# Attention values by plain fp32 products instead of split halves, and a deeper store-and-load ring for the exponentials

## What is computed

```python
xn = group_norm(x, gamma, beta)
xf = xn.reshape(B, n, C)                      # n = 1024 pixels, C = 128 channels
q = xf @ Wq + bq; k = xf @ Wk + bk; v = xf @ Wv + bv
attn = jnp.einsum('bnc,bmc->bnm', q, k) * scale
attn = jax.nn.softmax(attn, axis=-1)
out = jnp.einsum('bnm,bmc->bnc', attn, v)
out = out @ Wp + bp
return xn + out.reshape(B, H, W, C)
```

## Time and profile before

| | |
|---|---|
| median of 3 runs | 1132.37 us (1132.25 to 1133.01) |
| the profiled execution | 1129.47 us |
| its span in the trace | 1127.7 us |
| TensorE, VectorE, ScalarE, GpSimd busy | 86%, 80%, 66%, 63% of the span |
| mean granted TensorE clock | 0.964 of 2.4 GHz |

### The profile page before, as it was taken

How to read it: one execution, slowest core, us unless ns; L and a number is a source line. 1 busy time by engine, 2 the same in 40 slices (tenths; PEclk the granted TensorE clock), 3 DMA queues, 4 the chain that set the end, 5 groups by cost and what they waited for, 6 DMA issues and landing times.

```text
span 1127.7 us, 20253 instructions
## 1 busy us (share of the span) xinstructions
PE 965.2 (86%) x6068; PEld 852.9 (76%) x6068; DVE 905.2 (80%) x1628; ACT 749.6 (66%) x1402; POOL 714.5 (63%) x494
## 2 busy tenths in 40 slices
PE   5979988897979889898888989889798988999865
PEld 4867877686868778787777878778687887877754
DVE  7758977978888798787879888797988879887752
ACT  2467747767767676766767677676776767687532
POOL 5425684756848575694847659475675856665645
PEclk9999999999999999899998999999999998999987
DMA  6003637447262744637365363735636374456673
GB/s 103 3 1 94 175 86 188 122 141 181 83 184 84 201 134 117 173 87 207 85 180 152 105 158 102 204 103 158 167 91 169 96 199 124 118 159 191 192 209 94
DMA packets 177797, 152.87 MB, mean 136 GB/s; under 512 B 77792, under 2 KB 161248, under 8 KB 177760
## 3 DMA queue, kind: packets, MB, share of 16 engines
q1 hardware_dynamic: 176912, 152.03, 49.7%
q10 hardware_dynamic: 848, 0.39, 0.2%
HBM read 76.87 MB, written 75.50 MB: 135 GB/s over the span
## 4 chain that ended last, share of the span: by engine, by line
POOL 36%; issue 33%; DMA 6%; DVE 3%; PE 3%; SPq 1%; ACT 1%; POOLq 1%; DVEq 0%; ACTq 0%
POOL et_lo L1449 16%; POOL g_lo L1449 4%; POOL d L1455 4%; DMA e_by_keys<-e_blocks 3%; POOL r_tok L1508 3%; DMA e_blocks<-e 2%; POOL h_lo L1449 2%; POOL xn_lo L1449 2%; POOL t_lo L1449 2%; POOL r_tok L1511 2%; SPq L410 1%; DVE et_f L1934 1%; PE work L528 1%; PE work L530 1%; PE work L529 1%
## 5 line engine op out<-in xcount | busy, mean ns | idle before, releaser
L1449 POOL TENSOR_TENSOR et_lo<-et_f,et_hi 128x1024 fp32r<-128x1024 f32 x128 | 313.9, 2464 | 251.3 <-ACT et_hi L1073 251.3
L1934 DVE STREAM_TRANSPOSE et_f<-e_by_keys 128x1024 f32<-128x1024 f32 x128 | 157.5, 1237 | 103.6 <-DMA e_by_keys<-e_blocks 103.3
L528 PE MATMUL work<-t_lo,wc_hi 128*128 128x256 f32 x576 | 168.8, 293 | 10.3 <-DVE nm L1841 7.4
L528 PE MATMUL work<-et_lo,vv_hi 128*128 128x256 f32 x512 | 152.1, 297 | 16.5 <-POOL et_lo L1449 16.0
L530 PE MATMUL work<-t_hi,wc_hi 128*128 128x256 f32 x576 | 162.4, 282 | 0.0
L529 PE MATMUL work<-t_hi,wc_lo 128*128 128x256 f32 x576 | 162.0, 281 | 0.0
L1073 ACT ACTIVATE et_hi<-et_f 128x1024 fp32r<-128x1024 f32 x128 | 133.6, 1055 | 29.4 <-DVE et_f L1934 29.4
L529 PE MATMUL work<-et_hi,vv_lo 128*128 128x256 f32 x512 | 148.1, 289 | 0.0
L530 PE MATMUL work<-et_hi,vv_hi 128*128 128x256 f32 x512 | 148.0, 289 | 0.0
L1066 ACT ACTIVATE e<-ps_s,nm 128x1024 f32<-128x1024 f32 x64 | 71.4, 1115 | 80.2 <-DVE et_f L1934 76.7
L528 PEld LDWEIGHTS work<-t_lo,wc_hi 128*128 128x128 f32 x576 | 109.3, 190 | 17.1 <-DVE nm L1841 12.0
(11 more groups left out here) (183 smaller groups left out, 2743.3 us busy)
## 6 DMA issues: line engine op xcount, KB each, us to landing
e_blocks<-e SPq DMA_DIRECT2D x512, 128.0 KB, 2.6
e_by_keys<-e_blocks SPq DMA_DIRECT2D x128, 512.0 KB, 4.1
x_in<-in_x SPq DMA_DIRECT2D x64, 128.0 KB, 4.4
out<-r_tok SPq DMA_DIRECT2D x32, 256.0 KB, 2.4
w_up_t<-in_L_conv_w_up SPq DMA_DIRECT2D x1, 384.0 KB, 3.7
const<-in_const ACTq DMA_DIRECT2D x1, 166.0 KB, 4.5
y<-in_L_conv_w_up ACTq DMA_DIRECT2D x1, 128.0 KB, 4.5
y<-in_L_conv_w_qkv SPq DMA_DIRECT2D x1, 128.0 KB, 4.8
```

The lines of the kernel that those rows point to most:

```text
L528: te.matmul(dst, wh, xl, start=first, stop=False)
L1449: return pool.tensor_tensor(dst, full, hi, ALU.subtract)
L1934: dve.transpose(et_f[:, :, cols_].rearrange("p b (q j) -> p q b j", q=4), e_by_keys[t % 2][:, :].rearrange("p (q b j) -> p q b j", q=4, b= ...
```

## The change

`values` uses one plain fp32 product where it had three of fp32r, so the halves of the exponentials (`et_hi`, `et_lo`) and of the values (`vv_hi`, `vv_lo`) are no longer made; `vv_half` copies the values once, and `residual` needs one addition instead of two. The room of the two halves holds eight transposed tiles (`et`) instead of four, so `et_turn` of the next image waits only for the values that read the same two tiles. The blocks in memory get four places instead of two. `exp(n, t)` waits for the store of tile t - 2 and for the transpose of tile t - 3 (t - 2 for the last tile), where it waited for the transpose of t - 2. A tile is stored by one DMA of 512 KB, in another order of the queries within the tile, which `a_part` undoes with a strided write. The load of tile t follows the store of tile t + 1 on SyncE's queue. The lists of all engines and the plans of the banks are written anew. In TensorE's list for the fill, `make_weights` moves behind the first five convolutions. The diff, without the plans, the semaphores' declarations, the fill, the drain, and VectorE's and GpSimd's lists for a turn:

```diff
--- before.py
+++ after.py
@@ -203,17 +203,14 @@
         near = placed("near", [128, 2, 3, D], qq_at)
         kk_hi, kk_lo = (sb(f"kk_{p}", [128, PIX], F32R) for p in ("hi", "lo"))
         vv_at = region("vv_mem", 2 * TILES * 128)
-        vv_hi, vv_lo = (placed(f"vv_{p}", [128, TILES, 128], vv_at + 4 * TILES * 128 * k, F32R)
-                        for k, p in enumerate(("hi", "lo")))
+        vv_t = placed("vv_t", [128, TILES, 128], vv_at)
         nm1 = sb("nm1", [128, TILES])
         sum1 = sb("sum1", [128, TILES])
         rec1 = sb("rec1", [128, TILES])
         e = [sb(f"e_{k}", [128, PIX]) for k in range(2)]
         e_by_keys = [sb(f"e_by_keys_{k}", [128, PIX]) for k in range(2)]
         et_at = region("et_mem", 2 * TILES * HALF)
-        et_hi, et_lo = (placed(f"et_{p}", [128, TILES, HALF], et_at + 4 * TILES * HALF * k, F32R)
-                        for k, p in enumerate(("hi", "lo")))
-        et_f = placed("et_f", [128, TILES, HALF], et_at + 4 * TILES * HALF)
+        et = placed("et", [128, TILES, PIX], et_at)
         wc_f = placed("wc_f", [128, NT, 3, D], et_at)
         w_up1_t = placed("w_up1_t", [128, 3, D], et_at + 4 * NT * 3 * D)[:, :, :]
         diag = placed("diag", [128, 2, 3, 3, 128], et_at + 4 * (NT + 1) * 3 * D)
...
@@ -360,7 +355,7 @@
         wl1 = r_tok[:, :, :]
         wv_t = wl1[:, 2, :]
 
-        e_blocks = nc.dram_tensor("e_blocks", (2, 128 * PIX), F32, kind="Internal").ap()
+        e_blocks = nc.dram_tensor("e_blocks", (4, 128 * PIX), F32, kind="Internal").ap()
...
@@ -405,35 +400,33 @@
 
             def move_out(n, t):
                 sp.wait_ge(*e_ready.after(n, t))
-                blocks = e_blocks[t % 2].rearrange("(a j q m) -> q j a m", a=4, j=32, q=4)
-                for part in range(4):
-                    sp.dma_start(blocks[part], e[t % 2][32 * part:32 * (part + 1), :].rearrange("j (a m) -> j a m", a=4)) \
-                      .then_inc(written[t % 2].handle, 16)
+                sp.dma_start(e_blocks[t % 4].rearrange("(a q m) -> q a m", a=4, q=128),
+                             e[t % 2][:, :].rearrange("q (a m) -> q a m", a=4)).then_inc(written[t % 2].handle, 16)
 
             def move_in(n, t):
                 sp.wait_ge(*written[t % 2].after(n, t // 2))
-                sp.dma_start(e_by_keys[t % 2][:, :], e_blocks[t % 2].rearrange("(p c) -> p c", p=128)) \
+                sp.dma_start(e_by_keys[t % 2][:, :], e_blocks[t % 4].rearrange("(p c) -> p c", p=128)) \
                   .then_inc(moved[t % 2].handle, 16)
...
@@ -441,79 +434,79 @@
             def turn_program(it):
                 a, b, c, d = it, it + 1, it + 2, it + 3
                 move_out(a, 0)
+                move_out(a, 1)
                 move_in(a, 0)
-                move_out(a, 1)
+                move_out(a, 2)
                 move_in(a, 1)
-                move_out(a, 2)
                 move_out(a, 3)
                 move_in(a, 2)
+                move_out(a, 4)
                 move_in(a, 3)
-                load_x(d)
-                move_out(a, 4)
                 move_out(a, 5)
                 move_in(a, 4)
+                load_x(d)
+                move_out(a, 6)
                 move_in(a, 5)
-                move_out(a, 6)
                 move_out(a, 7)
+                store(a, 0)
                 move_in(a, 6)
                 move_in(a, 7)
-                store(a, 0)
                 store(a, 1)
...
@@ -680,13 +673,13 @@
 
             def values(n, j):
 
-                cols_ = slice((j % 2) * 256, (j % 2 + 1) * 256)
-                te.wait_ge(*et_lo_ready.after(n, 2 * j + 1))
-                te.wait_ge(*vv_lo_ready.after(n, 1))
+                pixels_ = slice(j * 256, (j + 1) * 256)
+                te.wait_ge(*et_ready.after(n, 2 * j + 1))
+                te.wait_ge(*vv_ready.after(n, 1))
                 te.wait_ge(*bank_free("pv", j, n))
                 for kt in range(TILES):
-                    mm = mm3(bank("pv", j, n)[:, 0:256], (vv_hi[:, kt, :], vv_lo[:, kt, :]),
-                             (et_hi[:, kt, cols_], et_lo[:, kt, cols_]), kt == 0, kt == TILES - 1)
+                    mm = te.matmul(bank("pv", j, n)[:, 0:256], vv_t[:, kt, :], et[:, kt, pixels_],
+                                   start=kt == 0, stop=kt == TILES - 1)
                 mm.then_inc(pe["pv"].handle, 1)
...
@@ -1051,31 +1044,28 @@
                 act.activation(kk_hi[:, k * HALF:(k + 1) * HALF], bank("kk", k, n)[:, :], ACT.Identity, bias=bk1) \
                    .then_inc(kk_hi_ready.handle, 1)
 
-            def vv_hi_half(n, k):
+            def vv_half(n, k):
                 act.wait_ge(*pe["vv"].after(n, k))
-                act.wait_ge(*v_sum_ready.after(n - 1, k))
+                act.wait_ge(*r_tok_ready.after(n - 1, k))
                 act.wait_ge(*pe["pv"].after(n - 1, 3))
-                act.activation(vv_hi[:, 4 * k:4 * k + 4, :], bank("vv", k, n)[:, :].rearrange("p (t c) -> p t c", t=4),
-                               ACT.Copy).then_inc(vv_hi_ready.handle, 1)
+                act.activation(vv_t[:, 4 * k:4 * k + 4, :], bank("vv", k, n)[:, :].rearrange("p (t c) -> p t c", t=4),
+                               ACT.Copy).then_inc(vv_ready.handle, 1)
 
             def exp(n, t):
                 act.wait_ge(*max1_ready.after(n, t))
-                act.wait_ge(*et_ready.after(n, t - 2))
+                act.wait_ge(*written[t % 2].after(n, t // 2 - 1))
+                act.wait_ge(*et_ready.after(n, t - 3 if t < TILES - 1 else t - 2))
                 if t % 4 == 0:
                     act.wait_ge(*rec1_ready.after(n - 1, t // 4))
                 act.activation(e[t % 2][:, :].rearrange("p (a b i) -> p b a i", a=4, b=TILES),
                                score_tile(n, t)[:, :].rearrange("p (b a i) -> p b a i", a=4, b=TILES), ACT.Exp,
                                bias=nm1[:, t:t + 1], accum_out=sum1[:, t:t + 1]).then_inc(e_ready.handle, 1)
 
-            def et_hi_tile(n, t):
-                cols_ = slice((t % 4) * 128, (t % 4 + 1) * 128)
-                act.wait_ge(*et_ready.after(n, t))
-                act.activation(et_hi[:, :, cols_], et_f[:, :, cols_], ACT.Copy).then_inc(et_hi_ready.handle, 1)
-
             def a_part(n, j):
                 act.wait_ge(*pe["pv"].after(n, j))
                 act.wait_ge(*pe["pj"].after(n, j // 2 - 1))
-                act.activation(a_all[:, (j % 2) * 256:(j % 2 + 1) * 256], bank("pv", j, n)[:, 0:256], ACT.Copy) \
+                pixels_ = a_all[:, (j % 2) * 256:(j % 2 + 1) * 256].rearrange("p (t i q) -> p t q i", t=2, q=4)
+                act.activation(pixels_, bank("pv", j, n)[:, 0:256].rearrange("p (t q i) -> p t q i", t=2, q=4), ACT.Copy) \
                    .then_inc(a_ready.handle, 1)
 
             def scale_biases():
...
@@ -1492,23 +1442,15 @@
                 minus(xn_lo[:, cols_], y[:, cols_], xn_hi[:, cols_].bitcast(F32)).then_inc(xn_lo_ready.handle, 1)
 
 
-            def et_lo_tile(n, t):
-                cols_ = slice((t % 4) * 128, (t % 4 + 1) * 128)
-                pool.wait_ge(*et_hi_ready.after(n, t))
-                minus(et_lo[:, :, cols_], et_f[:, :, cols_], et_hi[:, :, cols_].bitcast(F32)).then_inc(et_lo_ready.handle, 1)
-
             def residual(n, k):
                 four = slice(4 * k, 4 * k + 4)
-                pool.wait_ge(*vv_lo_ready.after(n, k))
+                pool.wait_ge(*vv_ready.after(n, k))
                 pool.wait_ge(*stored.after(n, k - 1))
                 if is_first(n) and k == 0:
                     pool.wait_ge(*w1_ready.after(0, 0))
                     pool.wait_ge(*vp_ready.after(0, 0))
                     pool.wait_ge(*biases_ready.after(0, 0))
-                pool.tensor_tensor(r_tok[:, :, :], vv_hi[:, four, :].bitcast(F32), vv_lo[:, four, :].bitcast(F32), ALU.add) \
-                    .then_inc(v_sum_ready.handle, 1)
-                pool.wait_ge(*v_sum_ready.after(n, k))
-                pool.tensor_tensor(r_tok[:, :, :], r_tok[:, :, :], bp_row[:, :].rearrange("p (a c) -> p a c", a=1)
+                pool.tensor_tensor(r_tok[:, :, :], vv_t[:, four, :], bp_row[:, :].rearrange("p (a c) -> p a c", a=1)
...
@@ -1910,12 +1812,6 @@
                 biased_lo(kk_lo[:, cols_], bank("kk", k, n)[:, :], bk1, kk_hi[:, cols_].bitcast(F32)) \
                     .then_inc(kk_lo_ready.handle, 1)
 
-            def vv_lo_half(n, k):
-                dve.wait_ge(*vv_hi_ready.after(n, k))
-                dve.tensor_tensor(vv_lo[:, 4 * k:4 * k + 4, :], bank("vv", k, n)[:, :].rearrange("p (t c) -> p t c", t=4),
-                                  vv_hi[:, 4 * k:4 * k + 4, :].bitcast(F32), ALU.subtract) \
-                   .then_inc(vv_lo_ready.handle, 1)
-
             def row_max(n, t):
                 dve.wait_ge(*pe["s"].after(n, t))
                 dve.wait_ge(*e_ready.after(n - 1, t))
@@ -1928,10 +1824,8 @@
                 if is_first(n) and t == 0:
                     dve.wait_ge(*g_lo_ready.after(1, 3))
```

(90 more changed lines are left out.)

706 lines of the change are left out of this document (311 added, 395 removed), and 58 rows, old and new, of tables (BANK_PLAN, DRAIN_PLAN, FILL_PLAN).

## The result

The change makes the kernel faster: 1008.53 us (median of 4 runs, 1007.76 to 1009.9) beside 1132.69 us for the kernel before on the same chip, a ratio of 0.8901 (95%: 0.8884 to 0.8918). I had forecast 1091 us with a range of 1060 to 1135.

The account below looks back on a forecast made before the run. No engine was full, so waits, mostly TensorE's, were taken as the bound. Twelve pipeline turns at -2.3 us (-28), the end -10 and the fill -2 took the profiled 1129.5 us to 1089; forecast 1091, range 1060 to 1135.

Parts of the forecast that it names:

- the sum of the waits: TensorE's waits for exp, `u`, `et_lo` and `vv_lo`, 5.1 us a turn: four fifths would go, -4.1 us.
- The term of -0.7 for the clock: TensorE: half of the 1.4 us a turn lost to low granted clock comes back with fewer gaps.
- The plain product: `values` on TensorE: 0.433 us a key tile instead of 0.356, adding 2.5 us a turn, up to 3.5.
- four passes: Products in `values`: by the skill's rule 0.476 us each, turn +3.8 us, 1107 us in all; chance 0.08.
- Line 1797: VectorE's update of `u`: stretched to 1919 ns by contention with GpSimd's `et_lo`; near 0.7 us without it.
- The loop of exps: ScalarE's exp, store, load, VectorE's transpose: a pair of tiles takes 7.7 us instead of 11.1.
- The end: Last image: faster exp pairs and no `et_hi` wait, less costlier values and unhidden earlier ones; together -10 us.
- The fill: Start of the kernel: five convolutions before `make_weights` gain 2 us, bounds 0 and 5.
- The single store: SP's queue: one 512 KB store issues sooner but lands later; 0.8 us less to 0.7 more, taken as zero.
- The orders: Lists of all engines and bank plans: moves not costed singly; 2 us allowed, for the fill.
- TensorE runs nearly full: Rival: all 5.1 us of waits, 1 us more and the low clock go; -5.0 a turn, 1057 us; chance 0.17.
- The waits come back elsewhere: Rival: load behind the next exp keeps VectorE waiting; about 0 a turn, some 1120 us; chance 0.19.

Follow-up runs that it names:

- a_load_next: Changed kernel, but in full turns, tiles 3 to 7, exp waits for the transpose of t-2 and each load follows its own store: 1139.85 us.
- p_halves_kept: Kernel before with one plain fp32 product of the high halves per key tile, all halves still made and waited for: 1131.76 us, ratio 1.0022.
- p_no_et_lo: p_halves_kept without GpSimd's low half of the exponentials, values waiting for ScalarE's high half instead: 1081.02 us, ratio 0.9568 to the kernel before.
- runs with six and ten tiles: Changed kernel with values summed over six key tiles, or ten (first two repeated), instead of eight: 994.81 and 1048.49 us.
- p_memset: p_halves_kept with GpSimd's low-half subtraction replaced by a constant fill of similar length that reads nothing: 1102.37 us, ratio 0.9760 to the kernel before.
- p_plain_only: Kernel before with the plain fp32 products alone, halves gone; loop, four stores and orders as before: 1077.02 us, ratio 0.9556.
- a_four_stores: Changed kernel with each tile stored by four transfers of 128 KB instead of one of 512 KB: 1054.95 us, ratio 0.9317 to the kernel before.
- r_ring_only: Kernel before with the new loop, four blocks and single store; halves and all orders but SyncE's as before: 1247.67 us, ratio 1.1054.
- pr_old_orders: Changed kernel's plain products and new loop, with the kernel before's engine orders (except SP) and bank plans: 1196.81 us, ratio 1.0607 to the kernel before.
- a_gpsimd_work: Changed kernel with eight unused GpSimd subtractions a turn put back about where the low halves stood: 1080.81 us, ratio 0.9586 to the kernel before.

## Why the prediction was wrong

**The step that failed is the sum of the waits:** "of the 5.1 us of named waits I take four fifths, -4.1, since a wait removed usually uncovers the next", and before it "The other 3.1 us of idle time a turn are waits of the local attention and of the output projection, which the change does not name". Idle time was to fall from 8.17 to 4.1 us a turn; it fell to 0.35. That is 3.7 us a turn, 41 us in eleven. The reason lies in how I had chosen the waits: by the engine that TensorE waited for last. The subtraction on GpSimd stretched VectorE's updates and delayed GpSimd's own later work, and an exp that waits holds ScalarE's list (a_load_next); both come out on TensorE as waits for `pt` or `a_all`, which I had put down as not concerned. In p_halves_kept, where the subtraction stands, and then in p_no_et_lo, where it alone is gone, these two are:
```profile
PE work L623 <- ACT pt L1032: 15.3, 11, 1.4
...
PE work L664 <- ACT a_all L1078: 5.6, 11, 0.5
```
```profile
PE work L664 <- ACT a_all L1078: 1.6, 6, 0.4
PE work L623 <- ACT pt L1032: 1.5, 3, 0.7
```
By parts: the plain products, with the halves' end, took the turn from 66.84 to 62.25 us, -4.6, where their terms made about +0.5 (+2.5, and four fifths of the 27.2 us for `u`, `et_lo` and `vv_lo`, -2.0); loop, single store and orders together took it on to 58.62, -3.6, where four fifths of the waits for exp made -2.1. The term of -0.7 for the clock belongs to both.

With the 24 us of busy time below, 12.2 of the fill and 5.8 of the end, less the 2.3 of a twelfth turn that I had counted, these 41 make 81 us; between the 1089 that I forecast for the profiled execution and its 1009.1 lie 80.

**The plain product.** Its price was right: 0.433 us a key tile predicted; the calls give 2 x 0.216 to 2 x 0.222 = 0.43 to 0.44. The Trainium skill (FP8 and Floating Point Precision, TensorE Precision Notes) says that true FP32 takes four passes; four at fp32r's 0.119 us would be 0.476 us a key tile, an estimate, and the calls show less. But I added the price to the path in full, +2.5 us a turn, and alone it costs nothing that can be told (ratio 1.0022). Of the busy time that I forecast, 58.67 + 2.5 - 0.7 = 60.5 us a turn, 58.27 was measured: 24 us in eleven turns. About 8 of the 24 are the clock, 1.00 instead of the half that I gave back. Where the other 16 went is not shown: busy time isn't the sum of the records' prices, as the runs with six and ten tiles show (3.53 us of records taken out lower it by 2.62, added they raise it by 3.15), but with the product alone it is 60.02 us, near the forecast, and it doesn't shrink where waits go with the subtraction (60.14 in p_memset, 60.07 in p_no_et_lo).

**Line 1797.** Right, in cause and size: 1919 to 715 ns, and p_memset shows that the subtraction's reading was it. What I did not see is what the time in GpSimd's queue costs, another 21 us.

**The loop of exps.** I had 7.7 us for a pair of tiles in the last image. The exps of one parity there, against the earlier trace rows:
```profile
958.66 1.11 ACT L1060 ACTIVATE e<-ps_t,nm 128x1024 f32<-128x1024 f32 x1 [1.82 <-DVE et L1828]
...
966.41 1.11 ACT L1060 ACTIVATE e<-ps_t,nm 128x1024 f32<-128x1024 f32 x1 [3.53 <-DVE et L1828]
...
974.13 1.11 ACT L1060 ACTIVATE e<-ps_t,nm 128x1024 f32<-128x1024 f32 x1
...
986.52 1.11 ACT L1060 ACTIVATE e<-ps_t,nm 128x1024 f32<-128x1024 f32 x1 [6.53 <-DVE et L1828]
```
7.75 and 7.72 us, and 12.4 for the last, which still waits for the transpose of t-2. The exact hit is luck: the exp at 974.13 shows no wait for a transpose but stood behind a copy of the values on ScalarE, and the exps of the other parity are 8.67 and 8.95 us apart:
```profile
961.16 1.11 ACT L1060 ACTIVATE e<-ps_s,nm 128x1024 f32<-128x1024 f32 x1 [1.29 <-DVE et L1828]
...
969.83 1.11 ACT L1060 ACTIVATE e<-ps_s,nm 128x1024 f32<-128x1024 f32 x1 [0.83 <-DVE rec L1836]
...
973.47 0.60 ACT L1051 ACTIVATE vv_t<-work 128x512 f32<-128x512 f32 x1 [2.43 <-PE work L647]
...
978.78 1.12 ACT L1060 ACTIVATE e<-ps_s,nm 128x1024 f32<-128x1024 f32 x1 [2.96 <-DVE et L1828]
```
A pair takes 7.7 to 9.0 us, then, clearly less than the 11.1 of before. The end gained 15.8 us where I had 10. The three intervals add up to 27.9 us (23.1 forecast, 33.3 at the pace of before), so the loop is some 5 of the 15.8, and where the rest lies was not traced. The fill gained 14.2 where I had 2; in p_plain_only it is 210.35 us, as before, so its gain came with loop, store and orders.

**The store and the orders.** The single store was costed at zero, an earlier issue set against a later landing; in the changed kernel it is worth 46 us (a_four_stores), with the loads behind a store issued 1.4 us later. The orders were 2 us in the sum. With the new loop they decide 188 us; I could not cost each move, and let that stand for a small number instead of a wide range.

**The rivals.** "TensorE runs nearly full" was the nearest, to which I gave 0.17. Its terms add up to -72 us, so to 1060, not 1057; it was too slow by the same busy time, by the fill and the end, and by another 1.7 us of idle time a turn that went. "The waits come back elsewhere" describes, in its mechanism, what r_ring_only and pr_old_orders do: the load behind the next exp keeps VectorE waiting, if the lists do not leave room for it.

## What to carry to other kernels

Follow a wait back past the engine that released it: an instruction removed from a queue frees all that stands behind it in that queue and every operation that it slowed beside it, even where its own consumer hardly waits. A longer pipeline between engines that work in order pays only with lists written for it, and can cost as much as it brings without them, so test the two together as well as singly. An engine's busy share is no bound by itself: take work off it and put work on, and see how much of the price comes back.

## What the runs showed of the hardware

- VectorE's update of 128x512 with both inputs in SBUF takes 683 ns on average in p_no_et_lo, without that work on GpSimd, 684 in p_memset beside GpSimd's fill, and 2123 in p_halves_kept beside its subtraction of two SBUF tiles, while the mean of the 128x1024 transposes stays at 1237 to 1243 in these runs. A step of 128x1 went from 281 to 1204 ns with such subtractions put back on GpSimd (a_gpsimd_work).
- ScalarE's copy of 128x256 into `a_all` takes 632 ns with the strided target of the changed kernel, 375 before; I had costed it at nothing, and no wait of TensorE's products in the turns shows it, only 5.2 us of its weight loads.
- Issuing four stores of 128 KB holds SP's queue 1.75 us, one of 512 KB 0.36, and they land after a median of 2.4 and 3.3 us: with four, the loads behind them were issued 1.4 us later, and the changed kernel took 46 us more.
